# Inverse norms by plain tensor-tensor operations on constant tiles, and cross scores by row halves

## What is computed

```python
def l2norm(t):
    return t / jnp.maximum(jnp.linalg.norm(t, axis=-1, keepdims=True), 1e-12)
...
q = l2norm(q) * qs
k = l2norm(k) * ksc
q = q * cos * scale + rotate_half(q) * sin * scale
k = k * cos * inv + rotate_half(k) * sin * inv
...
scores = jnp.einsum('bthd,bshd->bhts', q, k) / np.sqrt(HEAD_DIM)   # cross attention, 8 heads of 16
```

## Time and profile before

| what | value |
|---|---|
| median of 3 executions | 4879.15 us (4876.62 to 4883.68) |
| the profiled execution | 4873.85 us |
| its span, first to last instruction | 4872.0 us |
| mean granted clock of TensorE, share of full speed | 0.977 |
| PE, DVE, ACT, POOL busy | 90%, 81%, 63%, 61% of the span |

### The profile page before, as it was taken

How to read it: one execution, slowest core, us unless ns; L and a number is a source line. 1 busy time by engine, 2 the same in 40 slices (tenths; PEclk the granted TensorE clock), 3 DMA queues, 4 the chain that set the end, 5 groups by cost and what they waited for, 6 DMA issues and landing times.

```text
span 4872.0 us, 114175 instructions
## 1 busy us (share of the span) xinstructions
PE 4404.6 (90%) x33552; PEld 3380.6 (69%) x33552; DVE 3955.4 (81%) x8237; ACT 3046.9 (63%) x11581; POOL 2973.6 (61%) x3009
## 2 busy tenths in 40 slices
PE   7888887999998999989999989999899999899998
PEld 5676765777766777657777667777577776677775
DVE  5666666888878888778888788888788887888885
ACT  2444444777746777647777467777377775577773
POOL 2333334777746777647777467777377774577771
PEclk9999997999999999999999999999999999999999
DMA  4222220000000000000000000000000000000000
GB/s 138 75 84 70 80 74 18 0 0 0 0 19 6 0 0 0 0 24 1 0 0 0 19 6 0 0 0 0 24 1 0 0 0 18 6 0 0 0 0 18
DMA packets 75916, 82.96 MB, mean 17 GB/s; under 512 B 13622, under 2 KB 69396, under 8 KB 74836
## 3 DMA queue, kind: packets, MB, share of 16 engines
q1 hardware_dynamic: 75732, 80.87, 5.1%
HBM read 45.34 MB, written 35.52 MB: 17 GB/s over the span
## 4 chain that ended last, share of the span: by engine, by line
PE 53%; DVE 24%; issue 15%; ACT 5%; DVEq 1%; POOL 1%; DMA 0%; SPq 0%; ACTq 0%; POOLq 0%; PEldq 0%
PE bank_pair L1001 8%; PE bank L983 7%; PE bank L1016 7%; DVE pTl L1136 6%; PE bank L456 5%; PE bank L458 3%; PE bank L457 3%; DVE own_crossed L1092 3%; PE bank_pair L998 3%; PE bank L1008 3%; DVE own_crossed L1094 3%; DVE ss L1104 3%; PE bank L600 2%; ACT sc L625 2%; PE bank_pair L1211 2%
## 5 line engine op out<-in xcount | busy, mean ns | idle before, releaser
L1067 ACT ACTIVATE p<-bank_pair,mx 128x128 f32<-128x128 f32 x3072 | 1088.4, 366 | 654.4 <-DVE mx L1120 654.4
L1170 POOL TENSOR_TENSOR p<-p,ri 128x512 f32<-128x512 f32 x768 | 799.7, 1041 | 341.9 <-DVE ri L1112 341.9
L1166 POOL TENSOR_TENSOR rot<-own_crossed 128x512 f32<-128x512 f32 x768 | 983.3, 1280 | 29.4 <-DVE own_crossed L1094 29.4
L1120 DVE TENSOR_REDUCE mx<-bank_pair 128x4 f32<-128x512 f32 x768 | 528.7, 688 | 380.5 <-PE bank_pair L1001 369.8
L1160 POOL TENSOR_TENSOR rot<-rot,rn 128x512 f32<-128x512 f32 x768 | 804.2, 1047 | 32.4 <-DVE rn L1125 11.1
L983 PE MATMUL bank<-pTl,v_sb 128*64 128x128 f32 x6144 | 509.0, 287 | 217.8 <-DVE pTl L1136 217.3
L456 PE MATMUL bank<-wqkv_hi,xs_lo 128*128 128x512 f32 (+1 forms) x1536 | 668.4, 435 | 38.4 <-DVE own_crossed L1094 21.4
L1067 ACT ACTIVATION_READ_ACCUMULATOR p<-bank_pair,mx 128x1 f32 x3072 | 624.0, 203 | 0.0
L1045 ACT ACTIVATE qkT<-bank 128x512 f32<-128x512 f32 x768 | 456.4, 594 | 234.0 <-PE bank L974 234.0
L983 PEld LDWEIGHTS bank<-pTl,v_sb 128*64 128x64 f32 x6144 | 322.6, 137 | 375.5 <-DVE pTl L1136 235.7
L1001 PE MATMUL bank_pair<-qkT 64*128 64x128 f32 x6144 | 550.1, 298 | 0.0
(11 more groups left out here) (199 smaller groups left out, 8629.8 us busy)
## 6 DMA issues: line engine op xcount, KB each, us to landing
pos_scratch<-pos_sb SPq DMA_DIRECT2D x32, 1020.0 KB, 4.3
sc<-pos_scratch SPq DMA_DIRECT2D x32, 512.0 KB, 4.0
own_crossed<-in_L_ffn_Wqkv SPq DMA_DIRECT2D x6, 1536.0 KB, 6.7
ctx_sb<-in_ctx SPq DMA_DIRECT2D x32, 128.0 KB, 3.5
wo<-in_L_ffn_Wo SPq DMA_DIRECT2D x6, 512.0 KB, 7.1
mrow<-in_mask_BxS_fk SPq DMA_DIRECT2D x1, 2048.0 KB, 7.7
x_all<-in_x SPq DMA_DIRECT2D x4, 512.0 KB, 8.7
out<-res SPq DMA_DIRECT2D x8, 256.0 KB, 2.2
```

Source lines behind the costliest of these rows:

```text
L1067: last = nc.scalar.activation(p[:, j, h, :], s_ps[:, h % 2, h // 2 * T:(h // 2 + 1) * T], ACT.Exp, bias=mx[:, j, h % 2, h // 2:h // 2 + 1] ...
L1166: nc.gpsimd.tensor_tensor(rot[:, j4, :, :], own[:, j4, :, :], crossed[:, j4, :, :], ALU.add).then_inc(L["rot0"], 1)
L1170: nc.gpsimd.tensor_tensor(p[:, j, :, :], p[:, j, :, :], ri[:, j, :].unsqueeze(2).to_broadcast([128, G, T]), ALU.mult).then_inc(L["pn"], 1)
```

## The change

In the local attention the clamp becomes a tensor-tensor maximum with a tile `ss_least`, and the Newton step becomes four tensor-tensor operations instead of one such and two of the form scalar-tensor-tensor: root_sq; root_sq times ssc in place; a tile `onehalf` (filled with 1.5) minus that; times root0. The factors move into the immediates of Square and Ln and into the rotary tables. Two memsets before the first layer fill the new tiles.

In the cross attention `kexp` holds 4 copies instead of 8: copy h keeps the rows of head h and of head h + 4. The two score matmuls read rows 0 to 63 and rows 64 to 127 of `q2T` and `kexp`.

```diff
--- before.py
+++ after.py
@@ -77,8 +77,8 @@
     scale = np.concatenate([scale, scale], -1)
     cos, sin = np.cos(freqs), np.sin(freqs)
     sign = np.concatenate([np.ones(DL // 2, f), -np.ones(DL // 2, f)])[None, :]
-    q = f(QK_SCALE * ROOT_GAIN) * scale
-    k = f(ROOT_GAIN) / scale
+    q = f(QK_SCALE * ROOT_GAIN * math.sqrt(2.0)) * scale
+    k = f(ROOT_GAIN * math.sqrt(2.0)) / scale
     return np.ascontiguousarray(np.stack([cos * q, cos * k, sin * q * sign, sin * k * sign], 1).astype(f))
 
 
@@ -90,7 +90,7 @@
 
 def head_rows():
 
-    return (np.arange(D)[:, None] // DX == np.arange(HX)[None, :]).astype(np.float32)
+    return (np.arange(D)[:, None] // DX % (HX // 2) == np.arange(HX // 2)[None, :]).astype(np.float32)
 
 
 CONSTANTS = {
@@ -217,7 +217,7 @@
         bv_row = sb1("bv_row", [128, D])
         bo0_row = sb1("bo0_row", [128, D])
         box_row = sb1("box_row", [128, D])
-        heads = sb1("heads", [128, HX])
+        heads = sb1("heads", [128, HX // 2])
         mrow = sb1("mrow", [128, B, T])
         mcol = sb1("mcol", [128, B])
 
@@ -395,7 +395,7 @@
         ctx_sb = sb1("ctx_sb", [128, 2, CTX])
         ctxT = sb1("ctxT", [128, 2, T])
         kT = sb1("kT", [128, T])
-        kexp = sb1("kexp", [128, HX, T])
+        kexp = sb1("kexp", [128, HX // 2, T])
         v2 = sb1("v2", [128, 2, HX, DX + 1])
         q2T = sb1("q2T", [128, T])
         madd = sb1("madd", [128, T])
@@ -597,7 +597,8 @@
                     pe.wait_ge(S1["kexp"], u1 + 1)
                     pe.wait_ge(S1["pT"], u1 + 1)
                     for j in range(2):
-                        last = nc.tensor.matmul(W1b[j][:, :], q2T[:, :], kexp[:, HALF * j:HALF * (j + 1), :].rearrange("p h n -> p (h n)"), start=True, stop=True)
+                        rows = slice(HALF * DX * j, HALF * DX * (j + 1))
+                        last = nc.tensor.matmul(W1b[j][:, :], q2T[rows, :], kexp[rows, :, :].rearrange("p h n -> p (h n)"), start=True, stop=True)
                     last.then_inc(S1["S2_mm"], 1)
             pipeline(pe, B, 2, 3, emit, peeled=2)
 
@@ -831,8 +832,8 @@
                     pool.wait_ge(S1["kv"], u1 + 1)
                     if reused(first, k, 1, 1):
                         pool.wait_ge(S1["S2_mm"], u1)
-                    nc.gpsimd.tensor_tensor(kexp[:, :, :], kT[:, :].unsqueeze(1).to_broadcast([128, HX, T]),
-                                            heads[:, :].unsqueeze(2).to_broadcast([128, HX, T]), ALU.mult).then_inc(S1["kexp"], 1)
+                    nc.gpsimd.tensor_tensor(kexp[:, :, :], kT[:, :].unsqueeze(1).to_broadcast([128, HALF, T]),
+                                            heads[:, :].unsqueeze(2).to_broadcast([128, HALF, T]), ALU.mult).then_inc(S1["kexp"], 1)
                 if on(-1):
                     first_norm(u0 + 1, (k + 1) % 2)
                 if isinstance(first, int) and first + k < 4:
@@ -864,6 +865,8 @@
         xs_lo = sb("xs_lo", [128, 2, T], F32R)
         xs = (xs_hi, xs_lo)
         sq = sb("sq", [128, 2, 2 * G, DL])
+        ss_least = sb("ss_least", [128, 2, 2 * G])
+        onehalf = sb("onehalf", [128, 2, 2 * G])
         ss = sb("ss", [128, 2, 2, 2 * G])
         ssc = sb("ssc", [128, 2, 2, 2 * G])
         ss_log = sb("ss_log", [128, 2, 2, 2 * G])
@@ -1033,7 +1036,7 @@
                 if on(3) and k % 2 == 1:
                     m, j = P + 4 * i + (k - 3) // 2, (k - 3) // 2 % 2
                     act.wait_ge(L["clamp"], m + 1)
-                    nc.scalar.activation(ss_log[:, j, :, :], ssc[:, j, :, :], ACT.Ln, scale=ROOT_GAIN ** 2).then_inc(L["ss_log"], 1)
+                    nc.scalar.activation(ss_log[:, j, :, :], ssc[:, j, :, :], ACT.Ln, scale=2.0).then_inc(L["ss_log"], 1)
                     act.wait_ge(L["ss_log"], m + 1)
                     if reused(first, k, 3, 4):
                         act.wait_ge(L["rn"], m - 1)
@@ -1052,7 +1055,7 @@
                     act.wait_ge(L["proj_qk"], n(0) + 1)
                     if reused(first, k, 0, 2):
                         act.wait_ge(L["ssum"], n(0) - 1)
-                    nc.scalar.activation(sq[:, k % 2, :, :].rearrange("p h n -> p (h n)"), banks[k % 2][:, :], ACT.Square).then_inc(L["square"], 1)
+                    nc.scalar.activation(sq[:, k % 2, :, :].rearrange("p h n -> p (h n)"), banks[k % 2][:, :], ACT.Square, scale=ROOT_GAIN).then_inc(L["square"], 1)
                 if on(2):
                     act.wait_ge(L["proj"], n(2) + 1)
                     if reused(first, k, 2, 8):
@@ -1111,8 +1114,11 @@
                     dve.wait_ge(L["exp"], n(7) + 1)
                     nc.vector.reciprocal(ri[:, (k - 7) % 4, :], psums[:, (k - 7) % 4, :]).then_inc(L["ri"], 1)
                 if newton:
-                    dve.wait_ge(L["root_sq"], m + 1)
-                    nc.vector.scalar_tensor_tensor(root_err[:, jm, :, :], root_sq[:, jm, :, :], -0.5 * ROOT_GAIN ** 2, ssc[:, jm, :, :], ALU.mult, ALU.mult).then_inc(L["root_err"], 1)
+                    dve.wait_ge(L["root_sq"], 2 * m + 1)
+                    nc.vector.tensor_tensor(root_sq[:, jm, :, :], root_sq[:, jm, :, :], ssc[:, jm, :, :], ALU.mult).then_inc(L["root_sq"], 1)
+                if newton:
+                    dve.wait_ge(L["root_sq"], 2 * m + 2)
+                    nc.vector.tensor_tensor(root_err[:, jm, :, :], onehalf[:, :, :], root_sq[:, jm, :, :], ALU.subtract).then_inc(L["root_err"], 1)
                 if on(6):
                     dve.wait_ge(L["S"], n(6) + 1)
                     if reused(first, k, 6, 4):
@@ -1122,13 +1128,13 @@
                     dve.wait_ge(L["root_err"], m + 1)
                     if reused(first, k, 3, 8):
                         dve.wait_ge(L["rot"], n(3) - 6)
-                    nc.vector.scalar_tensor_tensor(rn[:, jr, :, :], root_err[:, jm, :, :], 1.5, root0[:, jm, :, :], ALU.add, ALU.mult).then_inc(L["rn"], 1)
+                    nc.vector.tensor_tensor(rn[:, jr, :, :], root_err[:, jm, :, :], root0[:, jm, :, :], ALU.mult).then_inc(L["rn"], 1)
                 if on(2) and k % 2 == 0:
                     m, jm = P + 4 * i + (k - 2) // 2, (k - 2) // 2 % 2
                     dve.wait_ge(L["ssum"], n(2) + 2)
                     if reused(first, k, 2, 4):
                         dve.wait_ge(L["ss_log"], m - 1)
-                    nc.vector.tensor_scalar(ssc[:, jm, :, :], ss[:, jm, :, :], 1e-24, None, ALU.max).then_inc(L["clamp"], 1)
+                    nc.vector.tensor_tensor(ssc[:, jm, :, :], ss[:, jm, :, :], ss_least[:, :, :], ALU.max).then_inc(L["clamp"], 1)
                 if on(8):
                     dve.wait_ge(L["T2"], n(8) + 1)
                     if reused(first, k, 8, 2):
@@ -1526,6 +1532,9 @@
             dve.wait_ge(zeroed, 1)
             nc.vector.nop().then_inc(part1_done, 1)
             dve.wait_ge(part1_done, 4)
+            nc.vector.memset(ss_least[:, :, :], 1e-24 * ROOT_GAIN ** 2).then_inc(ones_set, 1)
+            nc.vector.memset(onehalf[:, :, :], 1.5).then_inc(ones_set, 1)
+            dve.wait_ge(ones_set, 3)
             nc.vector.nop().then_inc(L["z"], 1)
             dve.wait_ge(rot_in, 16)
             with dve.Fori(0, LAYERS) as l:
```

## The result

The changed kernel takes **5040.98 us** (median of 4 executions, 5032.01 to 5045.98) against 4878.08 us (4876.62 to 4883.68) of the kernel before on the same chip: ratio 1.033, 95% interval 1.0311 to 1.0349, slower by 163 us. The forecast was 4970 us with a range of 4850 to 5085: right in sign and inside the range, but 71 us short, and outside the 4930 to 5010 us that the forecast gave itself without its rivals.

The account below looks back on a forecast made before the run. Prediction: PE busy 90%, DVE 81%, each stage read separately, small DVE operations standing still behind POOL. Profiled 4873.85 - 42 (row halves) + 132 (added operation) + 0.5 (memsets) = 4964, forecast 4970 us; range 4850 to 5085, without rivals 4930 to 5010.

Parts of the forecast that it names:

- Form costs nothing: Local attention: exchanging scalar-tensor-tensor for tensor-tensor operations costs nothing, as POOL holds both forms alike.
- Step A of the added operation: Local attention, first Newton step of a batch: POOL holds product and subtraction; net 0.66 to 0.7 us a batch, +132 us.
- Of these 0.5 us PE can use the 0.34 for which it idles.: Local attention: the clamp, held 0.16 instead of 0.66 us, gives PE back 0.34 of the 1.0 us lost.
- Step B: Local attention, second Newton step: the subtraction starts just before POOL's L1170; its 0.2 us is covered by a wait for PE.
- The clock, rival 1: Local attention: PE's longer pause lowers the clock in a third of 192 batches, +102 us, 5070 us; chance 0.25.
- Row halves: Cross attention: score matmuls on row halves run in pairs, 0.76 us less at full clock, about 1.6 at lower; -42 us taken.
- rows 8: Profile rows of the local scores: eight 128-column matmuls on alternating row halves take 0.71 us, four full ones 0.66.
- The 0.1 us for changing over: Cross attention: changing between row halves costs 0.1 us, so the score group gains 0.76 instead of 0.86.
- capped them at 0.66: Cross attention, batches of 21.37 us: L531 waits for ACT's exponentials and can move up by only 0.66 us.
- the number of batches that lose the low clock: Cross attention: if the low-clock stretch misses the score matmuls more often, all 32 batches approach 20.7 us, -47 us.
- Sum: Whole kernel: 4873.85 - 42 + 132 + 0.5 = 4964 us profiled, forecast as 4970 us; own range 4930 to 5010.
- rivals that would cost 100 us and more: Local attention: the falling clock, +102 us, chance 0.25; the second Newton step losing too, +115 us, chance 0.08.

Follow-up runs that it names:

- no_subtraction: Changed kernel without the operation 1.5 minus the product, the product itself going to rn: 4846.38 us (ratio 0.9925 to the kernel before).
- cross_only: Kernel before with only the row halves of the cross scores and the half-size key tile: 4843.53 us (ratio 0.992).
- experiments 2 and 3: 2 is no_subtraction; 3 is the changed kernel with POOL's addition waiting in the first Newton step until the subtraction is through: 4903.11 us (1.0048).
- experiment 5: Changed kernel with ACT copying v before it squares: 5087.14 us (ratio 1.0424 to the kernel before).
- experiment 6: Six extra unused matmuls in PE's pause: 4999.16 us in the changed kernel, 4950.35 us in that of experiment 5; PE's wait for oT also moved ahead.
- experiment 4: Changed kernel with both cross score matmuls reading the same rows 0 to 63: 5131.38 us (ratio 1.0523 to the kernel before).

## Why the prediction was right, and where it was short

- **Form costs nothing.** Right: no_subtraction lies 2.9 us from cross_only.
- **Step A of the added operation.** Right to the hundredths, and shown by experiments 2 and 3: the forecast had a product of 0.91, a subtraction of 1.2 that ends with the addition, an `rn` of 0.47 and a pause of 1.74, and these are the lengths in the rows. Of the batch it gave 0.66 to 0.7; the batches of 18.69 are 0.73 longer than those of 17.96.
- **"Of these 0.5 us PE can use the 0.34 for which it idles."** This step failed in every second batch. The clamp did become shorter and PE did start earlier, but the output L1019 then waited for ACT's copy of v (experiment 5), a wait that none of my rows of before showed. 78 × 0.3 = 23 us. I had followed DVE, POOL and PE and not ACT.
- **Step B.** Right: free, on a margin of 0.02 us, so with some luck.
- **The clock, rival 1.** It was no rival but a part: 34 intervals hit, not a third of 192, at 1.1 to 2.8 us each, about 44 us more than before; experiment 6 shows it by its cause. The forecast had it at zero or at +102, and the truth lay between. It is the largest miss of the sum.
- **Row halves.** 33.7 us against 42. The pairing is as read from rows 8, shown by experiment 4, and the group was forecast at 1.1 us. Net of the fill of 0.27 it went from 1.72 to 0.86 us. The Trainium skill (TensorEngine Tiling (Array Packing), Theoretical Speedup) gives up to 2x, and the trace, at 2.0 within the group, agrees. The 0.1 us for changing over, which I took from the local scores, is there too, but behind the group: the transpose L472 on 128 rows starts 1.06 us after the group's start, 0.20 more than 0.86, where it was 1.82, 0.10 more than 1.72; so the path gains 0.76, as forecast, and not 0.86. The batches at full clock gained 0.7 and 0.8 in turn, where I had capped them at 0.66. What was too high is the number of batches that lose the low clock: four stay at 23.0.
- **Sum.** Of the 71 us between forecast and result, about 44 are the clock, 23 the wait for v and 8 the cross scores; the rest, a few us the other way, is the batches near the ends of layers, which lose less than the others, and 0.73 for 0.69. The result lay inside the range because its upper end counted rivals that would cost 100 us and more; the sum itself, with its own 4930 to 5010, was too low.

What stays open: why the pause of 1.74 us at 1725.46 was followed by a lower clock and the one at 1687.78 was not; and whether operands in PSUM would spare the small operations POOL's hold, which was not tried.

## What to carry to other kernels

What follows is shown on this kernel alone. When DVE has small operations between the ones that PE waits for, look at where they end: if an operation of 0.17 us ends with POOL's, its price is POOL's remaining time, and a second one that depends on the first meets POOL's next operation whole. Order counts as much as number: taking the added operation out brought 195 us back, and moving one COPY ahead of two held operations brought another 139. After each pause made longer or shorter, read the granted clock beside the batch lengths, since a correct saving can come out as a loss.

## What was not expected of the hardware

- Useless matmuls in a pause made the kernel faster: 5041 to 4999 us, and 5087 to 4950.
- Shortening every batch by 0.2 to 0.4 us raised the number of intervals of 20 us and more, all with a mean granted clock of 0.92 or less, from 32 to 91 of 186.
- Two operations that meet pay very unevenly: POOL's grows by 0.02 us when DVE's small one starts 0.02 us ahead, DVE's by up to 1.04 us when it starts second.
- Two matmuls on the same 64 rows take 1.98 us, as two on 128 rows, but brought the lower clock in nearly every interval of the stage (0.86 in the window, against 1.00 and 0.93 by turns before).
